# A decoder's tail: mixtures paced by two and three scan steps a chunk, router weight multiplied into the tokens, normalisations with strip variances

## The chip, the cores and the metric

One core of a Trainium2 chip runs the whole program, all in fp32. The metric is the device time of one execution in microseconds. Before the change: 6497.38 us, the median of three runs (6492.47 to 6498.66).

## The reference, cut to what matters

The program is a two-layer decoder over x of 4 batches x 512 positions x 256 features, each sublayer followed by a layer normalisation. In order: a gated linear recurrence, an attention LSTM over 512 positions, a mixture of experts (8 experts, inner 256, the two best by the router), an RWKV-7 scan (16 heads of 16), a cross attention, and a second mixture (4 routed experts of inner 688, two of them per token, and a shared one that every token takes without a weight). What the change touches is this, for both mixtures:

```python
g = silu(x @ w_gate[e]);  u = x @ w_up[e]        # per expert e
y = sum_e weight[token, e] * ((g * u) @ w_down[e])
x = layernorm(x + y)                             # (x - mean) / sqrt(var + eps), no affine
```

The weight is a number per token and expert (zero where the expert is not chosen). It may stand on g * u or on x in the up product, since u is linear in x.

## The kernel before, in words

x lies transposed in SBUF as xT, features on partitions (2 chunks of 128) and 2048 tokens in columns, token = position x 4 + batch. The program has a recurrence phase, the long LSTM phase and the tail phase (`decoder_tail_phase`, from L1203), which alone is changed.

The tail works on blocks of 512 tokens (four blocks) and on tiles of 128 tokens, 32 positions each (sixteen tiles). The order is: an early normalisation of all blocks (`norm_phase`, L875), the first mixture on block 0 alone, then the RWKV scan with other work beside it, then what is left.

The scan is a loop of 16 x 32 = 512 steps on VectorE (`scan_slot`, L2041): five dependent operations a step on the 16x16 states. In certain steps of each tile it also does work for the next tile (transposes, sums) and for the output of the last. The other engines walk the same loop: TensorE computes the next tile's projections in step 0 of a tile (`project_columns`, which waits for `x_done`, the addition that VectorE makes in step 31 of the tile before), `project_inner` in step 3, `project_gate` in step 5, the output of the last tile in steps 22 and 25; ScalarE copies x in step 0, evacuates projections in step 1 (`project_products`, which waits for TensorE), and has further work in steps 4, 8, 10, 12, 15, 24, 26; GpSimd has elementwise work.

Beside it runs the background, as a Python generator per engine (`background`, L1427). After each scan step every engine's generator advances by one `yield`, so that the order of instructions in every queue is fixed when the program is built; the engines meet at run time by semaphores alone, and each queue is strictly in order. In the seventeenth round (c = 16), which has the last tile's output and no steps, the generators advance only at every fourth step. The background is: first mixture on block 1, keys and values of the cross attention from the context (four batches), first mixture on blocks 2 and 3, then for each block q: wait until its tiles are scanned (steps 160, 288, 416, and for the last block all), cross attention, second mixture. A chunk of the first mixture takes SLOTS = 3 steps, of attention and second mixture LATE_SLOTS = 2.

A mixture goes by chunks of up to 128 inner features: 16 chunks in the first (8 experts x 2), 30 in the second (the shared expert's 6 first, then 4 x 6; 115 rows each). Per chunk TensorE makes `gate` (L1556), `up` (L1567) and, one chunk later, `down` (L1582); ScalarE takes silu of gate into `gu`; VectorE multiplies by up (`gated`, L2083) and, for weighted chunks, by the router's weight (`weighted`, L2096). That weight has been spread over the partitions by a product with `pick` into `aux_ps` (L1574), once per expert. gate and up have one PSUM bank each, so gate of chunk n+1 waits for silu of n, and up of n+1 for VectorE's product of n. Chunk weights come through a ring of six buffers by DMA.

The router (L985): `sum_logits` and `turn_logits` on TensorE, a chain of 10 to 17 small operations on VectorE (`vector`) with one exponential on ScalarE in the middle (`keep_expo`), `turn_weights` on TensorE, `keep_rows` on ScalarE.

The normalisation (L73): means by a product with a constant matrix, deviation on VectorE, squares on ScalarE, variance by a product, root on ScalarE, reciprocal and result on VectorE, all on 512 columns. Its squares and deviations share the SBUF of `gu` and `gw`. norm_phase has another form of it: the variances of four groups of 128 columns are written to four strips of 32 partitions, so that root and reciprocal are 128x128, and then a product with `g.spread` spreads the reciprocal over the partitions (L926, L935, L958, L968, L977).

## Time and profile before

| | us |
|---|---|
| median of three runs | 6497.38 |
| profiled execution | 6499.01 |
| span of the profile | 6497.2 |
| first step of the scan | 4710.0 |
| last step of the scan begins | 6235.5 |
| scan's VectorE waits | 155.7 |
| VectorE busy, whole span | 3736.9 |
| TensorE busy, whole span | 5781.7 |

An engine's share over the whole span says little, as the LSTM phase takes two thirds of it. "Busy" of a matmul group counts its pipelined length. In the views a line number is that of the kernel before.

### The profile page before, as it was taken

To read this page: it belongs to the slowest core of one execution; us is meant where nothing else is said; L and a number is where in the kernel's file an instruction comes from. 1 tells how busy PE (TensorE), PEld (TensorE's weight loads), DVE (VectorE), ACT (ScalarE), POOL (GpSimd) and SP (SyncE) were. 2 spreads that over 40 slices of the span, in tenths; PEclk is the share of its full clock that TensorE was granted. 3 is DMA by queue.
4 is the path that set the end of the run, shared out by engine and by line. 5 is a ranking of instruction groups with operands and counts; after the bars stand their busy time and mean duration, and the time that the engine had idled before them with its cause. 6 is when DMAs were issued, how large, how long until landed. Compare 5 with 4: busy or idle time off the path is not lost. (4 is left out here: it accounts for less than half of the span.)

```text
span 6497.2 us, 369971 instructions
## 1 busy us (share of the span) xinstructions
PE 5781.7 (89%) x163920; PEld 3976.9 (61%) x163920; DVE 3736.9 (58%) x16359; ACT 2118.1 (33%) x7992; POOL 290.1 (4%) x779
## 2 busy tenths in 40 slices
PE   6899999999999999999999999999888779795979
PEld 2577777777777777777777777776434334443433
DVE  4355555555555555555555555555387998888852
ACT  3133333333333333333333333333122122222221
POOL 0000000000000000000000000000011011111000
PEclk8999999999999999999999999999898889897989
DMA  1100000000000000000000000000111101010111
GB/s 65 53 2 2 2 2 2 2 2 2 2 2 2 2 2 2 2 2 2 2 2 2 2 2 2 2 2 18 59 39 35 34 21 48 24 55 17 43 31 55
DMA packets 42841, 105.28 MB, mean 16 GB/s; under 512 B 7912, under 2 KB 9960, under 8 KB 42240
## 3 DMA queue, kind: packets, MB, share of 16 engines
q1 hardware_dynamic: 41312, 103.13, 5.2%
q10 hardware_dynamic: 1440, 1.06, 0.1%
q8 instruction: 45, 0.74, 0.1%
q14 instruction: 44, 0.36, 0.0%
HBM read 93.64 MB, written 10.52 MB: 16 GB/s over the span
## 5 line engine op out<-in xcount | busy, mean ns | idle before, releaser
L653 PE MATMUL lstm_part_ps<-lstm_keys,lstm_hid 128*4 128x128 f32 x32768 | 1036.1, 273 | 205.6 <-DVE lstm_hid L804 205.6
L669 PE MATMUL lstm_ctx_ps<-lstm_values,lstm_alpha 128*4 128x128 f32 (+1 forms) x49152 | 1092.6, 237 | 0.0
L653 PEld LDWEIGHTS lstm_part_ps<-lstm_keys,lstm_hid 128*4 128x4 f32 x32768 | 770.4, 86 | 440.2 <-DVE lstm_hid L804 426.0
L669 PEld LDWEIGHTS lstm_ctx_ps<-lstm_values,lstm_alpha 128*4 128x4 f32 x49152 | 895.8, 87 | 94.0
L831 DVE TENSOR_REDUCE lstm_neg_max<-lstm_part_ps 128x1 f32<-128x128 f32 x1024 | 298.4, 291 | 566.3 <-PE lstm_part_ps L653 566.3
L769 ACT ACTIVATE lstm_expo<-lstm_part_ps,lstm_neg_max 128x128 f32<-128x128 f32 x1024 | 376.4, 368 | 749.3 <-DVE lstm_neg_max L831 749.3
L612 PE MATMUL lstm_half_ps<-lstm_w_hid,lstm_hid 128*13 128x96 f32 x16384 | 591.0, 247 | 0.0
L789 DVE STREAM_TRANSPOSE lstm_gates<-lstm_half_ps 128x96 f32<-128x96 f32 x1024 | 289.9, 283 | 433.6 <-PE lstm_half_ps L612 409.5
L612 PE MATMUL lstm_half_ps<-lstm_w_attn,lstm_attn 128*13 128x96 f32 x16416 | 475.5, 247 | 0.7 <-ACT lstm_attn L782 0.7
L776 ACT ACTIVATE lstm_out_row<-lstm_ctx_ps,lstm_factor 128x128 f32<-128x128 f32 x512 | 188.4, 368 | 682.4 <-PE lstm_ctx_ps L669 682.4
L810 DVE COPY lstm_alpha<-lstm_part_ps 128x8 f32<-128x8 f32 x1024 | 176.6, 172 | 382.5 <-PE lstm_part_ps L676 382.5
L1567 PE MATMUL mix_up_ps<-xT,mix_ring 128*128 128x512 f32 (+2 forms) x736 | 357.1, 608 | 38.0 <-DVE mix_gated L2083 37.0
L1817 ACT ACTIVATE mix_gated<-mix_gate_ps 128x512 f32<-128x512 f32 (+2 forms) x184 | 109.9, 597 | 813.8 <-PE mix_gate_ps L1556 804.5
L612 PEld LDWEIGHTS lstm_half_ps<-lstm_w_attn,lstm_attn 128*13 128x13 f32 x16416 | 324.0, 94 | 75.9 <-ACT lstm_attn L782 45.9
L1582 PE MATMUL mix_down_ps<-mix_weighted,mix_ring 128*128 128x512 f32 (+2 forms) x736 | 359.2, 612 | 11.4 <-DVE mix_weighted L2096 11.4
L757 ACT ACTIVATE lstm_cell<-lstm_gates 128x12 f32<-128x12 f32 x1024 | 219.7, 215 | 447.3 <-DVE lstm_gates L789 447.3
L1556 PE MATMUL mix_gate_ps<-xT,mix_ring 128*128 128x512 f32 (+2 forms) x736 | 361.7, 615 | 1.3 <-DMA mix_ring<-in_mix_chunks 1.3
L856 DVE TENSOR_SCALAR lstm_out_row<-lstm_ctx_ps,lstm_factor 128x64 f32<-128x64 f32 x512 | 145.1, 283 | 365.0 <-PE lstm_ctx_ps L669 365.0
L612 PEld LDWEIGHTS lstm_half_ps<-lstm_w_hid,lstm_hid 128*13 128x13 f32 x16384 | 309.4, 94 | 61.9
L676 PE MATMUL lstm_part_ps<-lstm_ident,lstm_expo 128*128 128x128 f32 x1024 | 336.0, 328 | 8.2
L612 PE MATMUL lstm_half_ps<-lstm_xg,lstm_masks 128*13 128x96 f32 x8208 | 306.3, 249 | 9.1 <-DMA lstm_xg<-xg_rows 8.8
L766 ACT ACTIVATE lstm_tanh_c<-lstm_cell 128x4 f32<-128x4 f32 x1024 | 210.3, 205 | 318.1 <-DVE lstm_cell L797 318.1
(332 smaller groups left out, 8597.5 us busy)
## 6 DMA issues: line engine op xcount, KB each, us to landing
mix_ring<-in_sm_chunks SPq DMA_DIRECT2D x120, 358.0 KB, 3.0
mix_ring<-in_mix_chunks SPq DMA_DIRECT2D x64, 384.0 KB, 3.1
lstm_xg<-xg_rows SPq DMA_DIRECT2D x514, 16.0 KB
xg_rows<-lstm_xg_tile SPq DMA_DIRECT2D x16, 512.0 KB, 2.6
ctxT<-in_ctxT SPq DMA_DIRECT2D x1, 2048.0 KB, 14.8
out_xT<-xT SPq DMA_DIRECT2D x4, 512.0 KB, 3.8
xT<-in_xT SPq DMA_DIRECT2D x1, 1536.0 KB, 9.8
lstm_w_x<-in_lstm_w_x SPq DMA_DIRECT2D x1, 1024.0 KB, 7.8
```

Source lines behind the costliest of these rows:

```text
L612: mm = pe.matmul(ps[j * STRIP:j * STRIP + ROWS, :], rows, w[:, j * HID + cols.start:j * HID + cols.stop], start=start, stop=stop)
L653: mm = pe.matmul(part_rows(score_ps[part], b), hid[:, k, lo:lo + SPACE], keys[:, k, b * SRC + c * P:b * SRC + (c + 1) * P], start=(n == 0 ...
L669: mm = pe.matmul(part_rows(ctx_ps[n], b), alpha[:, b, c, SPACE - 1 - c:2 * SPACE - 1 - c], values[:, b * SC + c, ctx_cols[n]], start=(c == ...
L676: pe.transpose(turned_ps[part], expo[:, part, :], ident[:, :]).then_inc(alpha_turned, 1)
L757: act.activation(cell[:, k, 0:GATES - 1, :], by_batch(turned), ACT.Tanh).then_inc(half_tanh[k], 1)
L766: act.activation(tanh_c[:, k, :], cell[:, k, GATES - 1, :], ACT.Tanh, scale=0.5).then_inc(c_tanh[k], 1)
L769: act.activation(expo[:, part, :], score_ps[part], ACT.Exp, bias=neg_max[:, part:part + 1], accum_out=total[:, part:part + 1]).then_inc(ex ...
L789: dve.transpose(gates[:, k, :], half_ps[k]).then_inc(half_turned[k], 1)
L831: dve.tensor_reduce(neg_max[:, part:part + 1], score_ps[part], AX_X, ALU.max, negate=True)\
L1556: mm = pe.matmul(gate_ps[0:m, :], ring[:, at, k * e:k * e + m], token_block(i)[:, k, :], start=(k == 0), stop=(k == KC - 1))
L1567: mm = pe.matmul(up_ps[0:m, :], ring[:, at, lo:lo + m], token_block(i)[:, k, :], start=(k == 0), stop=(k == KC - 1))
L1582: mm = pe.matmul(down_ps[:, o_, :], ring[0:m, gn % RING, lo + o_ * P:lo + (o_ + 1) * P], gw[0:m, gn % 2, :], start=(n == 0), stop=(n == co ...
```

## The change

Four things change in the tail, beside small ones in their train.

1. Pace. SLOTS becomes 2 for everything, keys and values keep 3, and a mixture's chunk takes 2 steps if its number is even and 3 if it is odd.
2. Weights. `weighted` goes; `weigh_x` multiplies both feature chunks of the block by the spread weight into a new buffer `xw`, once per expert, and the up product of that expert's chunks reads xw. The spread is issued one chunk ahead, its stationary operand a column of the identity broadcast over 128 columns; `pick` and its load go.
3. Order of the router. In the first mixture the whole router comes before chunk 0 (three paces); in the second it comes after chunk 1 and 2 (turn_logits and VectorE's chain at chunk 1, exponential, turn_weights and rows at chunk 2).
4. Normalisation in strips, with inverse and result in steps of their own.

```diff
-SLOTS = 3
-LATE_SLOTS = 2
+KV_SLOTS = 3
+SLOTS = 2
+CHUNK_SLOTS = (2, 3)
...
+class StripNorm:
+    def variance(self, pe, n, ones):
+        pe.wait_ge(self.sq_ready, n + 1)
+        for k in range(KC):
+            for j in range(QUARTERS):
+                mm = pe.matmul(self.var_ps[j * STRIP:(j + 1) * STRIP, :], ones[:, 0:STRIP],
+                               self.sq[:, k, j * self.QT:(j + 1) * self.QT], start=(k == 0), stop=(k == KC - 1))
+        mm.then_inc(self.var_ready, 1)
+    def inverse(self, dve, n):
+        dve.wait_ge(self.std_ready, n + 1)
+        dve.reciprocal(self.rstd[:, :], self.rstd[:, :]).then_inc(self.rstd_ready, 1)
+    def spread(self, pe, n, strips):
+        pe.wait_ge(self.rstd_ready, n + 1)
+        for j in range(QUARTERS):
+            mm = pe.matmul(self.rstd_ps[:, j * self.QT:(j + 1) * self.QT], strips[:, j, :], self.rstd[:, :], start=True, stop=True)
+        mm.then_inc(self.rstd_spread, 1)
+    def result(self, dve, n, out):
+        dve.wait_ge(self.rstd_spread, n + 1)
+        return dve.tensor_tensor(out, self.d[:, :, :], over_chunks(self.rstd_ps), ALU.mult)
...
+        def chunk_slots(n, slots):
+            return 1 if slots == 1 else CHUNK_SLOTS[n % 2]
...  TensorE
-                    if n == 0 and x.at(i, 0) > 0:
-                        pe.wait_ge(ln.std_ready, norms_before(x, i))
-                    elif n > x.plain:
-                        pe.wait_ge(gu_ready, x.weighted_at(i, n))
-                    else:
+                    if gn > 0:
                         pe.wait_ge(gw_ready, gn)
+                    if x.opens_expert(n):
+                        pe.wait_ge(xw_ready, x.spread_at(i, n) + 1)
...
-                    pe.matmul(aux_ps[:, :], pick[0:x.x.routed, x.expert(n), :], router[x].weight_rows[:, :], start=True, stop=True)\
-                      .then_inc(spread_ready, 1)
+                    pe.matmul(aux_ps[:, :], ident[0:routed, e:e + 1].to_broadcast([routed, P]), router[x].weight_rows[:, :],
+                              start=True, stop=True).then_inc(spread_ready, 1)
...
+                if x.weighted(0):
+                    yield from pause(slots)
+                    router[x].turn_logits(pe, i, ident[:, :])
                     yield from pause(slots)
                     router[x].turn_weights(pe, i, ident[:, :])
-                    gate_up(2)
-                    down(1)
-                    yield from pause(slots)
-                for n in range(3, count):
+                    spread(0)
+                for n in range(count):
                     gate_up(n)
+                    if x.opens_expert(n + 1) and n + 1 < count:
+                        spread(n + 1)
+                    if n > 0:
+                        down(n - 1)
+                    if not x.weighted(0) and n == 1:
+                        router[x].turn_logits(pe, i, ident[:, :])
+                    if not x.weighted(0) and n == 2:
+                        router[x].turn_weights(pe, i, ident[:, :])
+                    yield from pause(chunk_slots(n, slots))
...  ScalarE
+                for n in range(x.count):
                     silu(n)
-                    yield from pause(slots)
+                    if not x.weighted(0) and n == 2:
+                        router[x].keep_expo(act, i)
+                        router[x].keep_rows(act, i)
+                    yield from pause(chunk_slots(n, slots))
...  VectorE
-                        dve.tensor_tensor(gw[0:m, at, :], gu[0:m, at, :], aux_ps[0:m, :], ALU.mult).then_inc(gw_ready, 1)
+                def weigh_x(n):
+                    dve.wait_ge(spread_ready, x.spread_at(i, n) + 1)
+                    if x.at(i, n) > 0:
+                        dve.wait_ge(mix_up_ready, x.at(i, n))
+                    dve.tensor_tensor(xw[:, :, :], block_x, over_chunks(aux_ps[:, :]), ALU.mult).then_inc(xw_ready, 1)
...
+                for n in range(x.count):
                     gated(n)
-                    weighted(n)
-                    yield from pause(slots)
+                    if not x.weighted(0) and n == 1:
+                        router[x].vector(dve, i)
+                    if x.opens_expert(n + 1) and n + 1 < x.count:
+                        weigh_x(n + 1)
+                    yield from pause(chunk_slots(n, slots))
                 dve.wait_ge(down_ready, x.at(i, x.count))
                 dve.tensor_tensor(block_x, down_ps[:, :, :], block_x, ALU.add).then_inc(added, 1)
                 yield from pause(slots)
                 ln.deviation(dve, norm_after_mixture(x, i), block_x)
                 yield from pause(slots)
+                ln.inverse(dve, norm_after_mixture(x, i))
                 yield from pause(slots - 1)
                 ln.result(dve, norm_after_mixture(x, i), block_x).then_inc(ln_done, 1)
```

## Rows read from the trace of the kernel before

**Rows 1.** The page's busy tenths of VectorE in 40 slices of the span.
```profile
DVE  4355555555555555555555555555387998888852
```

**Rows 2.** Windows (tiles 8, 3, 12): length, PE, PEld, DVE, ACT, POOL busy, clock, DMA.
```profile
5457.10:5562.90 105.80, 103.63 (x289) 49.41 (x288) 86.64 (x211) 23.40 (x42) 11.26 (x14) 0.98 0.16 46
4996.10:5087.80 91.70, 78.46 (x220) 37.79 (x220) 81.02 (x202) 19.57 (x35) 10.63 (x14) 0.96 0.16 47
5864.00:5949.10 85.10, 28.06 (x120) 19.57 (x119) 74.95 (x185) 12.02 (x26) 11.06 (x14) 0.67 0.09 32
```

**Rows 3.** Waits of VectorE in the scan: total us, times, longest us.
```profile
DVE mix_gated L2083 <- PE mix_up_ps L1567: 57.4, 27, 10.2
DVE tail_ln_rstd L121 <- ACT tail_ln_rstd L116: 22.7, 3, 9.3
DVE rw_kk_norm L1991 <- ACT rw_kk_sq L1754: 15.4, 1, 15.4
...
DVE rw_kk_norm L2002 <- ACT rw_kk_norm L1769: 10.4, 1, 10.4
```

**Rows 4.** The scan's first operation by line: count, shortest, median, longest ns, first, last start.
```profile
L2058 DVE TENSOR_TENSOR rw_terms<-rw_state,rw_sc x512: 493/553/1078, 4710.0 to 6235.5; 128x384 f32<-128x384 f32 x171
```

**Rows 5.** Timeline of VectorE, steps 256 to 258: start us, length us.
```profile
5457.08 0.55 DVE L2058 TENSOR_TENSOR rw_terms<-rw_state,rw_sc 128x384 f32<-128x384 f32 x1
...
5458.85 0.56 DVE L2058 TENSOR_TENSOR rw_terms<-rw_state,rw_sc 128x384 f32<-128x384 f32 x1
...
5461.88 0.55 DVE L2058 TENSOR_TENSOR rw_terms<-rw_state,rw_sc 128x384 f32<-128x384 f32 x1
```

**Rows 6.** Timeline of VectorE, step 448, with one multiply.
```profile
6055.23 0.55 DVE L2058 TENSOR_TENSOR rw_terms<-rw_state,rw_sc 128x384 f32<-128x384 f32 x1
...
6056.88 0.68 DVE L2086 TENSOR_TENSOR mix_weighted<-mix_gated,mix_up_ps 115x512 f32<-115x512 f32 x1
6057.48 0.55 DVE L2058 TENSOR_TENSOR rw_terms<-rw_state,rw_sc 128x384 f32<-128x384 f32 x1
```

**Rows 7.** Timeline of TensorE at the start of tile 8.
```profile
5461.14 1.95 PE L1481 MATMUL rw_bank_a<-rw_x_in,rw_w_r 128*128 128x128 f32 x16
...
5471.92 1.88 PE L1556 MATMUL mix_gate_ps<-xT,mix_ring 128*115 128x512 f32 x4
5473.64 1.88 PE L1567 MATMUL mix_up_ps<-xT,mix_ring 128*115 128x512 f32 x4
```

**Rows 8.** Groups by line, whole span: busy us, mean ns, then idle before.
```profile
L2096 DVE TENSOR_TENSOR mix_weighted<-mix_gated,mix_aux_ps 128x512 f32<-128x512 f32 (+2 forms) x160 | 110.1, 688 | 24.4 <-PE mix_aux_ps L1574 9.5 <-PE mix_down_ps L1582 2.3
L121 DVE RECIPROCAL tail_ln_rstd<-tail_ln_rstd 128x512 f32<-128x512 f32 x16 | 53.5, 3345 | 40.6 <-ACT tail_ln_rstd L116 40.6
...
L123 DVE TENSOR_TENSOR xT<-mix_weighted,tail_ln_rstd 128x1024 f32<-128x1024 f32 x16 | 19.7, 1232 | 0.6
```

**Rows 9.** Groups and timeline of the early normalisation, which has the strip form.
```profile
L968 DVE TENSOR_TENSOR xT<-mix_ln_d,mix_ln_rstd_ps 128x1024 f32<-128x1024 f32 x4 | 4.9, 1221 | 2.8 <-PE mix_ln_rstd_ps L935 2.8
L977 DVE RECIPROCAL mix_ln_rstd<-mix_ln_rstd 128x128 f32<-128x128 f32 x4 | 3.8, 951 | 2.8 <-ACT mix_ln_rstd L958 2.8
...
4547.59 0.64 PE L926 MATMUL mix_ln_var_ps<-mix_ln_sq,mean_mat 128*32 128x128 f32 x16 [1.01 <-ACT mix_ln_sq L951]
...
4548.84 1.16 PE L935 MATMUL mix_ln_rstd_ps<-mix_ln_rstd,spread 128*128 128x128 f32 x8 [0.60 <-DVE mix_ln_rstd L977]
```

**Rows 10.** Timeline: the context's first load, and the next block's router sum.
```profile
4885.41 0.58 SPq L1449 DMA_DIRECT2D mix_gated<-in_ctxT  x1
...
4941.65 1.88 PE L1026 MATMUL mix_aux_ps<-xT,mix_w_router 128*8 128x512 f32 x4 [1.19 <-ACT ca_values L1843]
```

**Rows 11.** ScalarE's table loads ahead of the normalisation's root, by line.
```profile
L116 ACT ACT_TABLE_LOAD x17 | 21.8, 1283 | 0.3
```

**Rows 12.** Timeline of VectorE behind the scan: the last tile's output.
```profile
6242.06 0.28 DVE L2179 TENSOR_TENSOR rw_terms<-rw_state,rw_sc 128x128 f32<-128x128 f32 x1
...
6253.45 0.60 DVE L2039 TENSOR_TENSOR xT<-xT,rw_bank_a 128x256 f32<-128x256 f32 x1 [7.22 <-PE rw_bank_a L1530]
```

More of the change, by code:

```diff
@@ L123, in result, with __init__, mean, deviation @@
         return dve.tensor_tensor(out, self.d[:, :, :], over_chunks(self.rstd[:, :]), ALU.mult)
+class StripNorm:
+    QT = NB // QUARTERS
+    def __init__(self, s, name, mean_ps, var_ps, d, sq):
+        self.mean_ps, self.rstd_ps, self.var_ps = mean_ps, mean_ps, var_ps[:, 0:self.QT]
+        self.d, self.sq = d, sq
+        self.rstd = s.sb(f"{name}_rstd", [P, self.QT])
+        self.mean_ready = s.sem(f"{name}_mean_ready")
+        self.d_ready = s.sem(f"{name}_d_ready")
+        self.sq_ready = s.sem(f"{name}_sq_ready")
+        self.var_ready = s.sem(f"{name}_var_ready")
+        self.std_ready = s.sem(f"{name}_std_ready")
+        self.rstd_ready = s.sem(f"{name}_rstd_ready")
+        self.rstd_spread = s.sem(f"{name}_rstd_spread")
+    def mean(self, pe, y, ones):
+        for k in range(KC):
+            mm = pe.matmul(self.mean_ps, ones, y(k), start=(k == 0), stop=(k == KC - 1))
+        mm.then_inc(self.mean_ready, 1)
+    def deviation(self, dve, n, y):
+        dve.wait_ge(self.mean_ready, n + 1)
+        dve.tensor_tensor(self.d[:, :, :], y, over_chunks(self.mean_ps), ALU.subtract).then_inc(self.d_ready, 1)
+    def squares(self, act, n):
+        act.wait_ge(self.d_ready, n + 1)
+        act.activation(self.sq[:, :, :], self.d[:, :, :], ACT.Square).then_inc(self.sq_ready, 1)
+    def variance(self, pe, n, ones):
+        pe.wait_ge(self.sq_ready, n + 1)
+        for k in range(KC):
+            for j in range(QUARTERS):
+                mm = pe.matmul(self.var_ps[j * STRIP:(j + 1) * STRIP, :], ones[:, 0:STRIP],
+                               self.sq[:, k, j * self.QT:(j + 1) * self.QT], start=(k == 0), stop=(k == KC - 1))
+        mm.then_inc(self.var_ready, 1)
+    def root(self, act, n, eps):
+        act.wait_ge(self.var_ready, n + 1)
+        act.activation(self.rstd[:, :], self.var_ps, ACT.Sqrt, bias=eps).then_inc(self.std_ready, 1)
+    def inverse(self, dve, n):
[9 more added lines that the diff above has]
+        return dve.tensor_tensor(out, self.d[:, :, :], over_chunks(self.rstd_ps), ALU.mult)
@@ L1140, in weighted, with opens_expert @@
         return n >= self.plain
+    def opens_expert(self, n):
+        return self.weighted(n) and n % self.x.chunks == 0
     def expert(self, n):
@@ L1430, in background @@
             for b in range(BATCH):
-                yield from keys_values(b, SLOTS)
+                yield from keys_values(b, KV_SLOTS)
             yield from mixture(FIRST, 2, SLOTS)
@@ L1435, in background @@
                 yield from until_scanned(engine, q)
-                yield from attention(q, LATE_SLOTS)
-                yield from mixture(SECOND, q, LATE_SLOTS)
+                yield from attention(q, SLOTS)
+                yield from mixture(SECOND, q, SLOTS)
         @block.sync
@@ L1554, in gate_up @@
                         pe.wait_ge(silu_ready, gn)
+                    if n == 0 and gn > 0:
+                        pe.wait_ge(ln_done, norms_before(x, i))
                     for k in range(KC):
@@ L1631, in mixture @@
                 yield from pause(slots)
+                ln.spread(pe, norm_after_mixture(x, i), g.spread)
                 yield from pause(slots)
@@ L1723, in attention @@
                 yield from pause(slots)
+                ln.spread(pe, norm_after_attention(q), g.spread)
                 yield from pause(slots)
@@ L1819, in mixture @@
                 router[x].keep_logits(act, i, (b_router if x is FIRST else no_bias)[:, :])
-                silu(0)
-                yield from pause(slots)
-                if not x.weighted(0):
-                    silu(1)
-                router[x].keep_expo(act, i)
-                yield from pause(slots)
-                router[x].keep_rows(act, i)
-                for n in range(1 if x.weighted(0) else 2, x.count):
+                if x.weighted(0):
+                    yield from pause(slots)
+                    router[x].keep_expo(act, i)
+                    yield from pause(slots)
+                    router[x].keep_rows(act, i)
+                for n in range(x.count):
                     silu(n)
-                    yield from pause(slots)
+                    if not x.weighted(0) and n == 2:
+                        router[x].keep_expo(act, i)
+                        router[x].keep_rows(act, i)
+                    yield from pause(chunk_slots(n, slots))
                 yield from pause(slots)
@@ L2098, in mixture @@
[L2098 to L2102 removed]
+                    dve.tensor_tensor(gw[0:m, at, :], gu[0:m, at, :], up_ps[0:m, :], ALU.mult).then_inc(gw_ready, 1)
+                def weigh_x(n):
[3 more added lines that the diff above has]
+                    dve.tensor_tensor(xw[:, :, :], block_x, over_chunks(aux_ps[:, :]), ALU.mult).then_inc(xw_ready, 1)
@@ L2103, in mixture @@
                 if x.weighted(0):
+                    yield from pause(slots)
+                    router[x].vector(dve, i)
+                    yield from pause(slots)
                     yield from pause(slots - 1)
-                    weighted(0)
+                    weigh_x(0)
                     yield
-                    first_late = 1
                 else:
-                    first_late = 1
-                for n in range(first_late, x.count):
+                    yield from pause(slots)
```

92 lines of the change are left out of this document (27 added, 65 removed).

## The prediction

> **What bounds the kernel now.** I read the page's slices first: VectorE is at half load for 28 slices, at 7 to 9 tenths in slices 30 to 38, and at 2 in the last [rows 1]. The change touches only the last third, so the question is what limits those slices. The windows by tile answer it [rows 2]. A tile is 32 steps of the scan. Tile 12, with little beside the scan, takes 85 us with TensorE busy 28; a tile with first-mixture chunks every third step takes 91.7 with TensorE at 78; a tile with second-mixture chunks every second step takes 105.8 with TensorE at 103.6. So the scan is a VectorE queue that waits for TensorE at places, and in the second mixture TensorE itself is the limit.
>
> The waits of VectorE inside the scan [rows 3] add up to 155.7 us (thirteen lines; four are shown). The first step begins at 4710.0, the last at 6235.5 [rows 4] and ends at 6237.6, 1527.6 us in all, so VectorE's own queue is 1372. Steps looked at singly give the unit prices [rows 5]: an empty step is 1.77 us (5457.08 to 5458.85), one with a gating and a weighting multiply 3.03 (5458.85 to 5461.88). A step with one multiply is 2.25 [rows 6]. So the first multiply costs 0.48 and the second 0.78: an operation costs its duration less 0.2 for the first of a step, plus 0.09 for a further one.
>
> Where the waits come from is seen at step 256, where tile 8 begins [rows 5, 7]. project_columns for the next tile starts on TensorE at 5461.1 and takes 10.8 us; gate, up, down are 1.72 each. A chunk issued behind it has its up product 18.5 us after the tile began, and VectorE, which gates every second step, stands 10.2 us for it, the longest of its line [rows 3]. TensorE's sum for that tile, 103.6 [rows 2], less 16 chunks of 5.16 and three spreads of 1.05, leaves 18 us for the scan: the 10.8, and 7 for project_inner (about 4), project_gate and the output.
>
> **VectorE work that leaves the scan.** (1) Weighting: of 160 multiplies [rows 8] 48 + 72 = 120 lie in the scan, at 0.78: -93.6. In their place come 8 x 3 + 4 x 3 = 36 products of the tokens, 128x1024 with a PSUM operand, for which the nearest row is the result of the early normalisation, 1.22 us [rows 9]: 33 as second operation at 1.31 and 3 in a step of their own at 1.02, +46.3. Net -47. From both sides: at 0.69 a piece and 1.4 per product it is -35, with full prices on both sides -55.
> (2) Normalisations: eleven are complete inside the scan. The reciprocal falls from 3.35 [rows 8] to 0.95 [rows 9], and stands in a step of its own, which saves another 0.2: 11 x 2.6 = -29.
> (3) Three gatings, the addition and the deviation of the block beside tiles 14 and 15 move behind the scan: 3 x 0.48 + 2 x 1.02 = -3.5.
> Sum: -79.
>
> At this place a rule of the Trainium skill speaks against the change. The row says that 128x1024 with the reciprocal spread in PSUM takes 1.221 us, against 1.232 from SBUF [rows 8, 9]. The Trainium skill ("VectorE: DVE Perf Modes", the section on the TRN2 errata) gives VectorE 62 cycles more when the source is in PSUM. By that rule 11 results and 36 products would cost some 3 us more in the scan; by the rows nothing.
>
> **Where the steps fall now.** With pace 2 and 3 in turn a first mixture takes 2+2+40+2+6 = 52 steps (63 before), a second one 75+2+6 = 83 (68 before), attention 28 as before, keys and values 12. So: F1 0-52, keys 52-64, F2 64-116, F3 116-168, attention0 168-196, S0 196-279, attention1 288-316, S1 316-399, attention2 416-444, S2 444-527. The scan has 512 steps, so 15 steps of S2 are left over; before, S2 ended with step 511.
>
> **Waits after.** For each tile start I lay TensorE's order against VectorE's. Two cases. If the last chunk ahead of the tile was freed a step earlier, project_columns starts with the tile and the next up is there at 13 us; if VectorE frees it in step 31 (or, as in the rows, step 0), up and down go first and it is 18.5 [rows 5, 7]. The chunk after that follows 5 to 9 us later, as project_inner and down lie between. VectorE reaches its gating at step 2, 3 or 4 after 5.3 + 1.77 a step, its second at 4 to 7, its third at 7 to 9. The largest lag counts.
> - Tiles 1, 3, 4 (first mixture), 7 and 12: odd chunk freed in step 31, 12.6 to 12.9 each; tile 8: 12.2; tile 11: 8.6. Sum 85. The slower pace helps little here, as the next two gatings still come within nine steps.
> - Tile 0 7, tile 5 (last addition behind the projections) 10, tile 6 (variance of the attention's normalisation) 9, tiles 9 and 13 (the attention starts with the tile) 12 each. Sum 50.
> - Tile 2: before, keys and values cost 15.4 + 10.4 [rows 3], and from the context's load to the router of the next block 56 us pass [rows 10], of which VectorE had 34 us of steps. Now F2's router stands in step 66, only 14 steps behind the normalisation (27 us of work), and asks for logits that lie behind four keys_values and project_columns; the router's exponential also lies behind ScalarE's copies. 33.
> - The router of S1 and S2 stands in step 320 and 448, the first of a tile. Its exponential comes on ScalarE behind silu of chunk 2, which needs a gate product behind project_columns (10.8 [rows 7]), and behind ScalarE's own project_products, and then a table load of 1.28 [rows 11]. VectorE stands about 13.5 us there, and 3.3 at the chunk before: 17 each, 34. In S0 only 3.
> - Small waits between chunks: 5.
> Sum 210 against 155.7: +54. The bounds: none of it worse than before (0), or every tile start of a chunk phase showing the scan's whole 18 us (+54 + 7 x 5.9 = +95).
>
> Scan: -79 + 54 = -25.
>
> **Before and behind the scan.** Block 0 of the first mixture runs alone. Its normalisation is serial: the variance, two products or 1.72 [rows 7], becomes 0.64, the reciprocal loses 2.4, the spread adds 1.16 [rows 9], the root on a quarter of the columns saves about 0.3 and 0.3 of start goes with the variance; that is -2.9, and ScalarE's table load (1.28 [rows 11]), hidden by the variance so far, shows a little: -2.8. Its router is now wholly ahead of chunk 0, but chunk 0 no longer runs at the slow clock before it: -1. One load less: 0. Together -4 (bounds -6, +2).
> Behind the scan three normalisations are serial: -2.6 each, -7.8. The leftover of S2 is half hidden: the last tile's output takes 12 us from 6242.06 until its addition at 6253.45 [rows 12], and two chunks fit beside it. What shows is down, addition and one normalisation, about 14, less the reciprocal and result (4.5) that stood there before: +9.3. Mixture 3 itself stays TensorE's, 1.72 per product; a product of the tokens (1.25) has spread, down and gate (4.5) as cover; if that were gone it would cost 1.25 four times. Together +1.5 (bounds -5, +10).
>
> **Sum.** -25 - 4 + 1.5 = -27.5. The profiled execution took 6499.0 us (span 6497.2); the median shown is 6497.4. 6499.0 - 27.5 = 6471.5, and against the median 6470. I say 6471.
>
> **Rivals.**
> A, the waits do not grow. For: more steps per chunk in the second mixture, where TensorE was full [rows 2]. Against: the order at the tile starts. -79 - 2.5 = -82: 6417 with nothing added; with half of +54 6444.
> B, slower: TensorE's backlog at the tile starts. Place: project_columns, project_inner, project_gate at the head of each tile, 18 us of TensorE with the output, with first-mixture chunks now at 5.7 us of TensorE for 2.5 steps (5.6 of VectorE where the steps are light). Price: the whole 18 shows in seven tiles, router and keys waits 10 longer: +95 + 10 instead of +54, 6471 + 51 = 6522. It decides from a mean wait of 16 us per tile start; the rows show 13.4 at most for a tile start today (10.2 + 3.2), in the fullest phase.
> C, no change: tile starts as costly as in the second mixture before (13.4) and the router and keys waits 8 longer each: +25 on the forecast, 6496.
> D, the change does not do what it says: the stationary operand as a broadcast column, or four strips one after the other. That would be 1.3 us in each serial variance, 5 us in all, inside the range.
>
> **How the numbers follow.** Forecast 0.57 (6450 to 6490), A 0.15, B 0.10, C 0.18. Forecast's own range is the tile starts by 3 us each (20) and the weighting's bounds. The range for 8 in 10 takes half of A and C: 6435 to 6502. What a measurement can tell from none is 0.2%, 13 us: faster needs under 6484. That is A, nearly all of the forecast and a little of C: 0.68; within 0.2% 0.20; slower 0.12.
>
> **What would show it.** Right: VectorE has 128x128 reciprocals at 0.95 and 36 products of the tokens near 1.22 in the scan; its busy time in the scan falls by some 75 us; its waits rise to about 210, of them about 33 at step 66, and at 320 and 448 a wait of 13 or more of the second router's first sum (L1079 of before) for ScalarE; the scan is 1500 us long. The stretch behind it is within 5 us of 259. Wrong: waits under 170 (A) or above 260 (B); a product of the tokens over 1.4; router waits under 5 us at steps 320 and 448, since then my order of ScalarE's queue is mistaken.

## The result, and the profile after

| | before | after |
|---|---|---|
| median of 20 runs, us | 6500.26 | 6490.18 |
| ratio (95% interval) | | 0.9982 (0.9975 to 0.9989) |
| a second series of the same kernel (e8, 11 runs) | 6499.92 | 6485.06, ratio 0.9977 (0.9968 to 0.9986) |
| profiled execution | 6499.01 | 6494.11 |

So 10 to 15 us are gained, where 27.5 were forecast. The first profile after is 10 us late already at the tail's first router sum (4565.33 against 4555.21), in phases that the change leaves alone; e8 below shows that this is scatter. From there on the two traces are compared in three stretches, to the first step of the scan, the scan, and the rest:

| stretch | before | after | forecast | found |
|---|---|---|---|---|
| router sum to first step | 154.7 | 148.7 | -4 | -6.0 |
| scan | 1527.7 | 1510.9 | -25 | -16.8 |
| behind the scan | 259.6 | 267.3 | +1.5 | +7.7 |
| sum | 1942.0 | 1926.9 | -27.5 | -15.1 |

The windows of the scan and of what lies behind it, before and after (columns as in [rows 2]):

```profile
4710.00:6237.60 1527.60, 1235.83 (x3667) 622.60 (x3666) 1319.08 (x3251) 359.90 (x634) 165.17 (x210) 0.90 0.12 35
6237.60:6497.20 259.60, 208.34 (x526) 89.49 (x526) 70.86 (x101) 43.52 (x71) 4.12 (x6) 0.91 0.16 47
```

```profile
4714.00:6224.90 1510.90, 1235.38 (x3839) 635.57 (x3838) 1245.64 (x3161) 358.14 (x632) 161.98 (x210) 0.88 0.11 35
6224.90:6492.20 267.30, 229.50 (x656) 102.93 (x654) 54.57 (x86) 49.49 (x79) 4.14 (x6) 0.93 0.14 46
```

In the scan VectorE's busy time (third) falls by 73 us, TensorE's (first) not at all, and the scan is only 17 shorter. TensorE's stays although 15 steps of work have moved behind the scan: over both stretches it is busy 1444 us before and 1465 after. Where VectorE's 73 us went is in the view of VectorE's waits in the scan, which answers to [rows 3] (total us, times, longest):

```profile
DVE mix_weighted L2136 <- PE mix_up_ps L1624: 99.7, 42, 8.7
DVE sm_router_total L1133 <- ACT sm_router_expo L1102: 29.9, 3, 13.2
DVE mix_router_logits L1127 <- PE mix_aux_ps L1086: 29.9, 2, 25.4
```

All lines of it sum to 222 us, against 155.7. L2136 is every gating, also those of the shared expert, which had a line of their own before:

```profile
DVE mix_weighted L2086 <- PE mix_up_ps L1567: 14.1, 4, 5.9
```

So the gating's wait for the up product went from 57.4 + 14.1 = 71.5 to 99.7 us. The prices of the operations themselves are as they were put; these groups (busy us, mean ns) answer to [rows 8, 9]:

```profile
L2143 DVE TENSOR_TENSOR mix_xw<-xT,mix_aux_ps 128x1024 f32<-128x1024 f32 x48 | 58.4, 1217 | 13.6 <-PE mix_aux_ps L1635 13.5
L177 DVE TENSOR_TENSOR xT<-mix_weighted,mix_gate_ps 128x1024 f32<-128x1024 f32 x16 | 19.5, 1220 | 14.9 <-PE mix_gate_ps L172 14.9
L167 DVE RECIPROCAL tail_ln_rstd<-tail_ln_rstd 128x128 f32<-128x128 f32 x16 | 15.2, 948 | 32.5 <-ACT tail_ln_rstd L163 32.5
```

The windows of tiles 8 and 3 after, as in [rows 2]:

```profile
5500.50:5588.10 87.60, 57.61 (x191) 31.61 (x190) 73.81 (x189) 17.32 (x32) 10.59 (x14) 0.80 0.11 39
5018.80:5119.80 101.00, 78.12 (x244) 38.99 (x243) 82.89 (x209) 22.84 (x40) 10.44 (x14) 0.83 0.10 31
```

Tile 3, first mixture, is 9 us longer than before, with TensorE no busier and VectorE by 2 us: its first gating waits 7.8 us and its second 3.8. From the tile's start TensorE works for 40 us without a pause, from 5022.5 to 5033.3 on the scan's projections, and idles only later; in the kernel before it was 38 us, and VectorE came for its products later. Tile 8 is 18 us shorter, but it holds less: its chunks come every 2.5 steps and end with step 279, and the last nine steps have no background. The router's wait that was forecast for step 320 is on the timeline of VectorE, behind the gating of chunk 1:

```profile
5698.90 0.17 DVE L1133 TENSOR_REDUCE sm_router_total<-sm_router_expo 128x4 f32<-128x16 f32 x1 [13.23 <-ACT sm_router_expo L1102]
```

### The profile page after: what moved, and what is told of

Read it like the earlier page. It is cut to its first block and busy times, and to the rows that moved or that the text cites. A ratio compares the mean times of both kernels' runs of the same rounds, so it can differ in the third digit from the quotient of the medians.

```text
span 6492.2 us, 370441 instructions
## 1 busy us (share of the span) xinstructions
PE 5807.1 (89%) x164240; PEld 4009.4 (62%) x164240; DVE 3645.8 (56%) x16247; ACT 2119.3 (33%) x7997; POOL 287.2 (4%) x779
## 5 line engine op out<-in xcount | busy, mean ns | idle before, releaser
L1624 PE MATMUL mix_up_ps<-mix_xw,mix_ring 128*115 128x512 f32 (+2 forms) x640 | 315.6, 617 | 43.3 <-DVE mix_weighted L2136 36.0
## 6 DMA issues: line engine op xcount, KB each, us to landing
ctxT<-in_ctxT SPq DMA_DIRECT2D x1, 2048.0 KB, 15.1
```

The source lines that it names most:

```text
L1624: mm = pe.matmul(up_ps[0:m, :], ring[:, at, lo:lo + m], xw[:, k, :] if x.weighted(n) else token_block(i)[:, k, :], start=(k == 0), stop=(k ...
```

## The experiments

Each ran beside the kernel before. In the table "gain" is the median less that of before run beside it; scan and the stretch behind it are read off the profile; waits are the sum of VectorE's idle gaps over 0.15 us in the scan, and own is the scan less the waits. e6 leaves the router weight out altogether. The profile is one execution: that of e10 was 10 us faster than its median, the others lie within 6 us of theirs, so a few us between two scans can be scatter.

| kernel | gain | ratio (95%) | scan | waits | own | behind |
|---|---|---|---|---|---|---|
| before | 0 | | 1527.7 | 155.7 | 1372 | 259.6 |
| after, first series | -10.1 | 0.9982 (0.9975 to 0.9989) | 1510.9 | 222.6 | 1288 | 267.3 |
| e8, after again | -14.9 | 0.9977 (0.9968 to 0.9986) | 1514.3 | 226.4 | 1288 | 267.3 |
| e1 after, old pace | -21.2 | 0.9965 (0.9952 to 0.9979) | 1522.3 | 228.9 | 1293 | 252.2 |
| e2 after, second mixture at 2 | +7.5 | 1.0013 (1.0004 to 1.0022) | 1546.5 | 251.8 | 1295 | 252.3 |
| e3 after, first mixture at 3 | -32.0 | 0.9951 (0.9938 to 0.9965) | 1456.6 | 170.7 | 1286 | 304.5 |
| e4 after, wide normalisations | +36.1 | 1.0054 (1.0041 to 1.0068) | 1545.2 | 232.7 | 1313 | 281.2 |
| e5 before, strip normalisations | -30.6 | 0.9950 (0.9936 to 0.9964) | 1510.4 | 167.9 | 1343 | 250.0 |
| e6 before, no weighting multiply | -36.8 | 0.9943 (0.9929 to 0.9956) | 1496.4 | 211.4 | 1285 | 259.1 |
| e7 after, exponential earlier | -16.5 | 0.9975 (0.9964 to 0.9985) | 1513.4 | 225.5 | 1288 | 265.3 |
| e9 e5, spare steps used | -33.2 | 0.9947 (0.9934 to 0.9961) | 1504.3 | 164.4 | 1340 | 249.4 |
| e10 e5, second mixture's tokens weighted | -35.0 | 0.9946 (0.9933 to 0.9960) | 1497.5 | 193.5 | 1304 | 249.3 |
| e11 e10 and e9 | -48.9 | 0.9922 (0.9909 to 0.9936) | 1489.9 | 190.2 | 1300 | 249.8 |
| e12 after, projections cut in two | -27.5 | 0.9960 (0.9946 to 0.9974) | 1495.8 | 209.9 | 1286 | 267.5 |
| e13 e11 and e12 | -45.9 | 0.9931 (0.9917 to 0.9944) | 1489.8 | 192.6 | 1297 | 250.0 |
| e14 after, second mixture's block 2 at 2 | -10.8 | 0.9982 (0.9973 to 0.9991) | 1530.5 | 237.3 | 1293 | 250.2 |

### The pace: e1, e2, e3

```diff
-CHUNK_SLOTS = (2, 3)
+FIRST_SLOTS = (3, 3)      # e1, e3; (2, 3) in e2
+SECOND_SLOTS = (2, 2)     # e1, e2; (2, 3) in e3
...
-            yield from mixture(FIRST, 1, SLOTS)   # and 2, 3
+            yield from mixture(FIRST, 1, 3)       # in e1 and e3
```

> The changed kernel with the pace of before: a first-mixture chunk and pause every 3 steps, a second-mixture chunk every 2; weighting on the tokens, strip norms and router order stay. Theory T (VectorE is one queue; work taken out counts except where TensorE is full, and in the second mixture at 2 steps a chunk TensorE is full): of the weighting the first mixture saves only 6 us, the second's 41 turn into waits, the norms save some 25, and nothing of the second mixture is left over behind the scan: 6475 (6465 to 6485), scan about 1500, its waits 190 to 200, behind the scan about 253. Rival A (waits do not grow when VectorE's work goes): waits 156, 6415. Rival P (the slower pace is what gains in the changed kernel, the VectorE edits bring nothing): 6500.

> The changed kernel with its second mixture at 2 steps a chunk throughout (first mixture still 2 and 3 in turn). Theory T: each second mixture inside the scan goes back to a TensorE-bound tile of some 103 us for 16 chunks, +12 to +14 us a block, +40 in the scan; what was left over behind the scan is gone, -15: 6515 (6500 to 6525). Rival: TensorE is no limit and the leftover is all that counts: 6475.

> The changed kernel with its first mixture at 3 steps a chunk and pause (second still 2 and 3 in turn). Theory T: the waits of tiles 1, 3, 4 fall from 15 to 16.5 us each to those of before (5.0, 7.3, 2.4) and the keys' wait at tile 2 by 10; 7 more steps of the last second mixture are left over behind the scan (+4): 6490 - 35 + 4 = 6460. Rival (the waits at tile starts come from TensorE's order and not from its load): waits of these tiles stay at 15, 6494.

e1 came at 6479.7, e2 at 6508.3, e3 at 6468.8, e1 and e2 within their ranges. In e1 only the sum is right: its scan took 1522 us where I expected about 1500, its waits were 229 and not 190 to 200. The pace is two edits of opposite sign. At 2.5 steps a chunk the first mixture costs: from after to e3 tiles 0 to 4 shrink from 505.7 to 460.4 us. Of these 45 us 32 are waits, and 13 are work of VectorE that comes in later tiles; 37 us more than after stand behind the scan. The waits of tiles 1, 3 and 4 fell from 15 to 16.5 us each to 7.1 to 7.8, about as theory T had it. The second mixture gains by the slower pace: back at 2 steps (e2) the scan is 32 to 36 us longer, though 15 us come back behind it. With both at the old pace (e1) the kernel is 6 to 11 us faster than after, so the new pace as a whole loses.
In e3 I had the leftover wrong: three first mixtures of 66 steps and the keys end at step 210, and three second ones at 2.5 steps then leave 31 steps over, not 22. That is why the stretch behind its scan is 52 us longer than in e1 and e2, which leave nothing over, and it still was 17 to 22 us faster than after.

### The normalisations: e4 and e5

e4 puts the 512-column form back into the kernel after; e5 is the kernel before with StripNorm in place of LayerNorm and nothing else (the first gate product of a mixture, the keys and the attention wait for the normalisation's result, as in the change).

```diff
 e4, StripNorm (rstd is 128x512 again, and result reads it directly)
-            for j in range(QUARTERS):
-                mm = pe.matmul(self.var_ps[j * STRIP:(j + 1) * STRIP, :], ones[:, 0:STRIP],
-                               self.sq[:, k, j * self.QT:(j + 1) * self.QT], start=(k == 0), stop=(k == KC - 1))
+            mm = pe.matmul(self.var_ps, ones, self.sq[:, k, :], start=(k == 0), stop=(k == KC - 1))
...
     def spread(self, pe, n, strips):
-        pe.wait_ge(self.rstd_ready, n + 1)
...
-        mm.then_inc(self.rstd_spread, 1)
+        pass
 e5, on the kernel before
-        ln = LayerNorm(s, "tail_ln", gate_ps[:, :], up_ps[:, :], d=gw, sq=gu)
+        ln = StripNorm(s, "tail_ln", gate_ps[:, :], up_ps[:, :], gw, gu)
```

> The changed kernel with normalisations on 512 columns again (variance by two products, root and reciprocal 128x512, no spread), in the same steps. Theory T (a saved reciprocal counts in full on VectorE's queue): +2.4 x 11 = +26 in the scan, +1.9 x 4 outside: 6490 + 34 = 6524. Rival (the 2.4 us go into waits that follow for TensorE anyway): waits fall by the same amount, 6505 or less.

> The kernel before with the strip normalisations alone (inverse and result in steps of their own; pace, weighting and router order as before). Theory T (a saved reciprocal counts in full, as e4 showed from the other side, +46.8): 6500 - 45 = 6455, scan -33, behind the scan -7. Rival W (at 2 steps a chunk TensorE is full, so what VectorE saves there becomes waiting): half of it, 6478.

By the gains e4 lies 46 us above after's first series and 51 above e8, more than the 34 of theory T: the scan is 31 to 34 us longer, with 24 us of VectorE's own time and 6 to 10 of waits, and 14 us come behind it and 3 ahead. e5: -30.6, between theory T's -45 and the rival's -22, of which -17.3 in the scan, -9.6 behind it, -3.3 ahead of it. Of the 29 us that VectorE saves in the scan, 12 turned into waits. So the strip normalisations by themselves gain two to three times what the whole change does, and the other edits together lose 16 to 20 us of it. Without the strips (e4) they lose 36 us against the kernel before. The parts don't add up to the whole, so the worth of the strips depends on what stands beside them: 31 us in the kernel before, 46 to 51 in the kernel after.

### The weighting: e6 and e10

```diff
 e6, on the kernel before: TensorE, up, then VectorE
-                    elif n > x.plain:
-                        pe.wait_ge(gu_ready, x.weighted_at(i, n))
...
-                        dve.tensor_tensor(gu[0:m, at, :], gu[0:m, at, :], up_ps[0:m, :], ALU.mult).then_inc(gu_ready, 1)
...
-                        dve.tensor_tensor(gw[0:m, at, :], gu[0:m, at, :], aux_ps[0:m, :], ALU.mult).then_inc(gw_ready, 1)
+                        dve.tensor_tensor(gw[0:m, at, :], gu[0:m, at, :], up_ps[0:m, :], ALU.mult).then_inc(gw_ready, 1)
 e10, on e5, TensorE
+                    if x.opens_expert(n):          # the second mixture alone
+                        pe.wait_ge(xw_ready, x.tokens_at(i, n) + 1)
-                        mm = pe.matmul(up_ps[0:m, :], ring[:, at, lo:lo + m], token_block(i)[:, k, :],
+                        mm = pe.matmul(up_ps[0:m, :], ring[:, at, lo:lo + m],
+                                       xw[:, k, :] if x is SECOND and x.weighted(n) else token_block(i)[:, k, :],
```

> The kernel before with the weighting multiply left out (weights have no effect on the output; the spread product and all waits for it stay), to see what taking 120 operations of 0.78 us off VectorE inside the scan is worth at the old pace. Theory T as in the prediction (work out counts in full but at tile starts): -94 + 20 of new waits = 6426. Rival W (TensorE, or the chain gate, silu, product, up, already sets the pace of those chunks, and VectorE's saving turns into waits): scan -30 at most, 6470, and waits of 210 or more.

> The kernel of e5 with the router weight multiplied into the tokens in the second mixture alone (first mixture, pace and router order as before). 72 weighting multiplies leave the scan, 12 products of the tokens come, 41 us of VectorE. Theory W (TensorE full at 2 steps a chunk): nearly all of it becomes waits, -5: 6464, waits up from 168 to about 200. Rival T (work out counts in full): 6428.

e6 is the plainest of all. VectorE's own time falls by 87 us, the waits grow by 56, the scan is 31 shorter. That is rival W, 7 us under its 6470. Its waits of the gating for the up product, 71.5 us before, are now

```profile
DVE mix_weighted L2083 <- PE mix_up_ps L1565: 115.8, 43, 11.6
```

and its windows have the same TensorE as before, 1222.6 against 1235.8:

```profile
4710.50:6207.00 1496.50, 1222.63 (x3668) 618.07 (x3666) 1241.26 (x3131) 359.80 (x634) 166.07 (x210) 0.91 0.12 36
```

Tile 8, full of chunks at 2 steps, took 105.9 us before and 102.2 here, with TensorE busy 101.8 and waits up from 15.3 to 22.3: of 10.7 us of VectorE's work 3.7 were gained. A full TensorE is not needed for the loss. In tile 3 of e6, with TensorE busy 83.1 of 90.1 us, 1.6 of 8.3 us were gained, in tile 1, with 64.8 of 90.1, 0.7 of 6.2. e10 says the same of the second mixture alone: 38 us of VectorE gone, 26 us of waits come, 13 us of scan gained (4.4 in the gains against e5's, within what two such series differ by; e10's profile is the fast one).
At this place the Trainium skill can be read both ways ("Perfetto Trace Analysis", Identifying the Most-Contended Engine, and Optimization Strategy): it says to optimise first the engine with the highest occupancy (TensorE it judges by other measures than busy time), which in this scan is VectorE, 1319 of 1528 us; e6 shows that two thirds of what is taken off it comes back as waiting. The same page says that one gap that repeats through a stretch can mean too little SBUF or PSUM for the next tile. That would fit gate and up, which have one bank each, but no run here gave them a second one, so this rival stands untested.

### The tile start, order or load: e7, e12, e13

```diff
 e7, on after, ScalarE
-                    if not x.weighted(0) and n == 2:
+                    if not x.weighted(0) and n == 1:
                         router[x].keep_expo(act, i)
+                    if not x.weighted(0) and n == 2:
                         router[x].keep_rows(act, i)
 e12, on after (and e13, on e11), TensorE and ScalarE
                 if has_next and t == 0:
                     project_columns(c + 1)         # now r, w and a alone
+                if has_next and t == 2:
+                    project_rkv(c + 1, ("k", "kk", "r", "v"))
...
+                if has_next and t == 3:
+                    project_rkv(c + 1)             # the copies of k, kk, r, v
```

> The changed kernel with the second router's exponential on ScalarE behind silu of chunk 1 and no longer behind chunk 2's. Theory T (VectorE stands 13.2 us at steps 320 and 448 for ScalarE's order, since silu of chunk 2 waits for a gate product behind project_columns, and project_products stands in between): those two waits fall to under 3 each, the gating of chunk 2 takes back some 3: 6490 - 14 = 6476. Rival (TensorE's backlog at the tile start is the limit, the exponential only shows it): the waits move to the gating of chunk 2, 6488.

> The changed kernel with project_columns cut in two: its first half (receiver columns and the two small ones, some 5 us) stays in step 0, the eight row products (k, kk, r, v) go to step 2, ScalarE's copies of them to step 3. TensorE's and VectorE's work is the same. Theory O (the waits at tile starts come from the order: up of the next chunk lies behind all of the 10.8 us): the first gating wait of each chunk tile falls from some 8 to 3, a little comes back at the second: -35 over the scan, 6450. Rival L (TensorE's load over the tile is what counts, the order only says where it shows): waits within 10 us of the 223 to 226 there are, 6480 or more.

e7 took the router's wait away, and its sum did not move: 225.5 us, where e8 has 226.4 and the first profile 222.6. In its waits the exponential is nearly gone and the gating has what it had:

```profile
DVE mix_weighted L2137 <- PE mix_up_ps L1624: 131.0, 45, 9.1
...
DVE sm_router_total L1133 <- ACT sm_router_expo L1102: 0.8, 3, 0.3
```

That is the rival of e7: ScalarE's order only showed TensorE's backlog. e12 shows the same at tile 8, where the split lets a chunk's products go ahead of the rows'. VectorE's gatings of steps 258 and 260, first of after, then of e12:

```profile
5513.32 0.69 DVE L2136 TENSOR_TENSOR mix_weighted<-mix_gated,mix_up_ps 115x512 f32<-115x512 f32 x1 [7.57 <-PE mix_up_ps L1624]
5518.48 0.69 DVE L2136 TENSOR_TENSOR mix_weighted<-mix_gated,mix_up_ps 115x512 f32<-115x512 f32 x1 [1.04 <-PE mix_up_ps L1624]
```

```profile
5484.52 0.69 DVE L2148 TENSOR_TENSOR mix_weighted<-mix_gated,mix_up_ps 115x512 f32<-115x512 f32 x1 [0.65 <-PE mix_up_ps L1630]
5496.59 0.69 DVE L2148 TENSOR_TENSOR mix_weighted<-mix_gated,mix_up_ps 115x512 f32<-115x512 f32 x1 [7.95 <-PE mix_up_ps L1630]
```

8.6 us in both, one gating later. Likewise at step 320: the router's wait fell from 13.2 to 6.3, and 6.8 came at the gating of step 325; and so at step 448. In tile 11 the waits even rose, from 11.4 to 13.6. The split did gain 2.5 to 4 us each, against e8, in tiles 0, 5, 6, 9 and 13, where a router, an addition or a normalisation stands at the tile's start in place of the chunks.

In tiles 1, 3, 4, 7 and 12 no wait moved by more than 0.5 us, but they are no test. No background work of TensorE falls between steps 0 and 2 there, so the eight products that were put off still go ahead of the next chunk, as in tile 3 of e12:

```profile
5017.52 1.89 PE L1538 MATMUL rw_bank_c<-rw_w_v,rw_x_in 128*128 128x256 f32 x8
5019.24 1.88 PE L1621 MATMUL mix_gate_ps<-xT,mix_ring 128*128 128x512 f32 x4
```

In all 13 to 17 us of waits went and 13 to 17 us of time. That is half of what theory O wanted and more than rival L allowed: neither holds alone. Load is shown for tiles 8, 10, 11 and 14, order for 0, 5, 6, 9 and 13, and for the five others it stays open.

> The kernel of e11 (strip normalisations, token weighting and spare steps in the second mixture, first mixture as before) with project_columns cut in two as in e12. Theory L (TensorE's load sets the waits, a cut only moves some of them): 6449 - 10 = 6439, waits 190 to 180. Rival O (the order at the tile start is what costs): -30, 6419. Other rival (the cut delays the rows' chain and gives nothing in light first-mixture tiles): 6449.

On e11 the same split gains nothing (-45.9 against -48.9, waits 192.6 against 190.2), by its time the last of the three expectations. Here it does change TensorE's order, at 12 of the 15 tile starts, tiles 1 and 3 of the first mixture among them, so at this pace the waits are shown to come from load.

### Pace by the steps to spare: e9, e11

In e5 the background stands idle from step 393 to 416, since block 2 isn't scanned yet. e9 and e11 spread the second mixture's chunks of blocks 0 and 1 over those steps; block 2 stays at 2, so that nothing is left over.

```diff
+        def chunk_slots(x, i, n, slots):
+            return 2 + (n >= 3 and ((i == 0 and n % 2 == 1) or (i == 1 and n % 4 == 3))) if x is SECOND and slots > 1 else slots
```

> The kernel of e5 (before with strip normalisations alone) with the idle steps ahead of step 416 given to the second mixture's chunks: block 0 at 2 and 3 steps in turn, block 1 with a third step at every fourth chunk, blocks 2 and 3 at 2. Nothing is left over behind the scan. Theory W (at 2 steps a chunk TensorE is full and a slower pace takes waits away; from e2 against the changed kernel some 12 us a block): 6469 - 8 - 4 = 6457. Rival (with two multiplies a chunk VectorE is the bound at 2.5 steps too): 6469.

> The kernel of e10 with the pace of e9. Theory W: where chunks come every 2.5 steps TensorE has room and VectorE's saving counts there: e9's 6457 less some 12 us for two blocks, less 5: 6440. Rival (the saving goes into the tile starts there too): equal to e9.

With two multiplies a chunk the slower pace gives 6 us of scan (e5 to e9) and, in the gains, only 2.6, where I expected 12; with one multiply it gives 8 us of scan (e10 to e11) and 14 of gain. Between e9 and e11, the same pace with and without the weighting multiplies of the second mixture, lie 14 us of scan and 16 of gain, of 40 us of VectorE. At 2 steps (e5 to e10) it was 13 of scan and 4 of gain. The scans agree and the medians don't, so that the weighting on the tokens is worth more at the slower pace is not shown. e11 came 9 us above its forecast of 6440, and it is the fastest kernel of all: 6448.7 us, 0.9922 of before (0.9909 to 0.9936). Tile 8, e5 above and e11 below:

```profile
5450.00:5555.70 105.70, 103.68 (x290) 49.41 (x289) 86.53 (x211) 23.44 (x42) 11.65 (x14) 0.98 0.16 46
```

```profile
5441.20:5535.30 94.10, 88.16 (x262) 43.11 (x261) 77.65 (x196) 22.30 (x40) 10.77 (x14) 0.98 0.17 49
```

### The leftover: e14, and the second profile: e8

```diff
+        def chunk_slots(x, i, n, slots):
+            return 1 if slots == 1 else 2 if x is SECOND and i == 2 else CHUNK_SLOTS[n % 2]
```

> The changed kernel with the second mixture's block 2 alone at 2 steps a chunk, so that none of it is left over behind the scan. Theory (the leftover shows with 15 us behind the scan, by e2, where the prediction had 9.3; inside the scan the block costs some 12 more at TensorE's full load): behind the scan 252, scan +12 to +14, 6485 to 6488 against 6485 and 6490 of the changed kernel, no change. Rival (the leftover was pure loss): 6475.

> The changed kernel again, unchanged, for a second profile of it. Theory N (the 10 us by which its first profile is later at the tail's first router sum is scatter of the recurrence and the LSTM phase): that sum at 4555 to 4560 here, the stretch behind it again 1927. Rival (a lasting effect of the change on earlier phases): again at 4565.

e14: behind the scan 250.2 (-17.1), in the scan +16 to +20 (+12 to +14 expected); nothing in sum. e8: router sum at 4558.1 and the stretch behind it 1930.4, so the lateness of the first profile is no effect of the change. Over the sixteen profiles that moment lies between 4552.7 and 4565.3; the two highest besides the first are e13 and e14, which ran on a chip of their own. There the kernel before was slowest too (6503.44), so a part of the scatter may be the chip's; no run separates it.

## Why the prediction was wrong

The direction and the prices of the operations held; the sum of the waits and the stretch behind the scan did not. By its steps:

- **VectorE work that leaves the scan, -79**: right. Own time fell by 84 us (1372 to 1288): normalisations -29.6 (e5; -29 forecast), weighting and router order -49 (e1 less e5; -47), moved out -5 (-3.5). (The sum's low bound for the weighting was miscounted: 120 at 0.69 less 36 at 1.4 is -32 and not -35; full prices give -57 and not -55. Neither moves the forecast.) Products of the tokens 1.217 us and reciprocals 0.948 were as in [rows 9]. The results, now with the reciprocal in PSUM, took 1.220 against 1.232, so the longer PSUM start of which the Trainium skill speaks ("VectorE: DVE Perf Modes", the section on the TRN2 errata) doesn't show here either.
- **Waits, +54**: the step that failed. They are +67 (222 us), and in e8 +71. The tile starts were close: tiles 1, 3, 4, 7, 12 waited 11.7 to 12.3 in their first ten steps (12.6 to 12.9 forecast), tile 8 10.7 (12.2), tile 11 11.4 (8.6), together 82 where 85 were forecast; tiles 0, 5, 6, 9, 13 56 (50); step 320 and 448 13.2 for the router (13.5), tile 2 with the keys and the router 31 to 32 (33). The term that was mis-sized is "small waits between chunks: 5": what waits beyond a tile's first ten steps, routers and tile 2 apart, is 25.9 us (12.6 before). I looked at tile starts alone, and the gatings between them wait too.
A second thing is wrong in kind, though it does not show in this sum. I took VectorE's saved work in full and added the waits from the order at each tile start as a term of its own. The runs at the pace of before show them coupled: VectorE walks faster, TensorE's work doesn't shrink, and the wait takes up the difference. e6: 87 us of work out, 56 of waits in. e5 to e1: 49 out, 61 in, so weighting on the tokens with the new router order (and nine more steps of first mixture) makes the scan 12 us *longer* at the old pace. e7 moved its waits and got them back beside; e12 did so in four tiles.
- **The pace**: the new tile starts of the first mixture were priced and came (tiles 1, 3 and 4: 12.3, 11.9, 11.9 us, where before they had 5.0, 7.3, 2.1); what the prediction lacked there were the waits later in these tiles, 8 us together. It never priced the faster first mixture by itself: e3, with 3 steps, is 17 to 22 us faster than after. The second mixture's slower pace does gain, 32 to 36 us of scan less 15 behind (e2).
- **Before the scan, -4**: -6.0 (e8 also -6.0).
- **Behind the scan, +1.5**: +7.7. The three serial normalisations gave -9.6 (e5; -7.8 forecast). The leftover was mis-sized: 9.3 in the sum, 17 by e14. "Two chunks fit beside" the last tile's output was the error. The output's chain took 17.8 us from the last state to its addition, where it takes 12.7 in e14, since its gatings wait for up in between; and the normalisation of the leftover comes behind it. TensorE stands idle there before each of its products (1.32, 2.40 and 1.59 us), the granted clock from 6245.70 to 6256.30 is 0.71 on the mean, between its levels of 2.4 and 1.2 GHz, and the spread took 2.1 us and not the 1.16 of [rows 9]. That is no matter of this place: in 15 of the 16 normalisations of the kernel after, and of e5, the spread ran at a granted clock of about 0.50, the 1.2 GHz level, and took 2.07 or 2.08 us. VectorE and TensorE there in the kernel after:

```profile
6228.92 0.69 DVE L2136 TENSOR_TENSOR mix_weighted<-mix_gated,mix_up_ps 115x512 f32<-115x512 f32 x1 [2.90 <-PE mix_up_ps L1624]
...
6239.23 0.69 DVE L2136 TENSOR_TENSOR mix_weighted<-mix_gated,mix_up_ps 113x512 f32<-113x512 f32 x1 [3.58 <-PE mix_up_ps L1624]
6242.73 0.62 DVE L2091 TENSOR_TENSOR xT<-xT,rw_bank_a 128x256 f32<-128x256 f32 x1 [2.82 <-PE rw_bank_a L1587]
```

```profile
6252.78 2.07 PE L172 MATMUL mix_gate_ps<-tail_ln_rstd,spread 128*128 128x128 f32 x8 [1.59 <-DVE tail_ln_rstd L167]
```

- **Sum**: 8 us short in the scan, 6 behind it, 2 better ahead of it. That leaves -15.1 by the first pair of traces and -11.6 by e8's.
- **Rivals**: C, no change, had the right neighbourhood by the wrong reason (costlier tile starts, which did not come). A, waits that don't grow, is out: they are 222 us. B's 18 us per tile start did not come. D is out in its own terms: a variance in four strips took 0.64 to 0.71 us, or 1.08 at the lower clock, and one product with the broadcast column 0.69 us at the median, as one with pick did before. That the time came within the range is in part luck: VectorE saved 5 us more than forecast, which hid a part of the waits.
- **Its own signs** of being right: six came, namely reciprocals at 0.95, products of the tokens at 1.22, 73 us less busy (75), 222 to 226 us of waits (210), 31 to 33 at steps 63 to 70, 13.2 at steps 320 and 448. Two did not: the scan is 1511 to 1514 us long (1500), and the stretch behind it is 8 us from before's and not within 5 of 259. None of the signs of being wrong came. They tested where waits come, not what they are worth.

Open stays how the 25 us by which e1's scan is longer than e10's divide: between them lie the first mixture's weighting on the tokens, the two routers' order and nine more steps of first mixture. No run separates them.

## What to carry to other kernels

Where two in-order engines meet at single buffers, a saving on one is worth only what the other's backlog leaves: a third of it in e6. The partner's share of a whole stretch doesn't tell how much: in e6 3.7 of 10.7 us counted in tile 8, where TensorE is busy 101.8 of 102.2 us, and only 0.7 of 6.2 in tile 1, where it is busy 64.8 of 90.1. Lay out instead, from each place where the queues meet, when the partner has its product ready and when the engine that was made faster comes for it; for the tile starts here that came within 4 us of 85. Do it for every meeting, not for the large ones alone. A change made of several edits can hide a loss in a gain: here the normalisations alone gained 31 us, and the rest gave back half of it or more; price them one by one, and from both ends, since they needn't add up. A wait that is moved out of one instruction and found again at the next, with the same sum, is load, not order; but see first that the edit did change the order there, which in e12 it did not in five tiles.

## What the runs showed of the hardware

Across sixteen profiles of the same recurrence and LSTM code its end lies within 12.6 us (4552.7 to 4565.3), which is as much as this change is worth; a single pair of spans (6497.2 and 6492.2) would have said 5 us. The kernel before, run again beside each group of experiments, had medians from 6497.66 to 6503.44.

The spread of the tail's normalisation, eight 128x128 products, took 2.07 or 2.08 us at a granted clock of about 0.50 in 15 of 16 normalisations after, and 1.16 at the full clock in the early one [rows 9]. TensorE had stood idle for 0.5 to 4.7 us just before each of the 15, and for 0.1 us before the one that took 1.26.
